# A macaron stack on one Trainium2 core: linear attention rewritten as one sequence of 128 query steps that also carries the projections, the FFN work and, on TensorE, a step's jobs ahead of its output products

## The reference

```
x = x + 0.5 * quant_ffn(layernorm(x))      # int8 weights and activations, 256 -> 256
x = x + linear_attn(layernorm(x))          # below
x = x + 0.5 * quant_ffn(layernorm(x))
x = x + 0.5 * routed_ffn(layernorm(x))     # top 128 of 1024 rows, 256 -> 1024 -> 256, gelu
x = x + attn(layernorm(x))                 # softmax, 16 heads of 128
x = x + 0.5 * routed_ffn(layernorm(x))
```

```
sq, sk = elu(q) + 1, elu(k) + 1
kv = einsum('bhsd,bhse->bhde', sk, v)
qkv = einsum('bhsd,bhde->bhse', sq, kv)
norm = einsum('bhsd,bhd->bhs', sq, sk.sum(axis=2))
return (qkv / (norm[..., None] + 1e-6)).transpose(...).reshape(b, s, H * D) @ Wo.T
```

## Time and profile before

| | us |
|---|---|
| Median of 3 runs | 3826.03 (3824.67 to 3826.09) |
| The profiled execution's own time | 3823.92 |
| Its span, from the first to the last instruction | 3822.3 |
| Setup | 0 to 18 |
| QA, four batches | 18 to 98.5 |
| Linear stage | 98.5 to 749.3 |
| Lead-in of attention (QB, FA and X of batch 0) | 749.3 to 883.1 |
| Attention's slots | 883.1 to 3722.6 |
| Tail, FB of batch 3 | 3722.6 to 3822.3 |

### The profile page before, as it was taken

One profiled execution on the slowest core, in us unless ns is written; L12 is line 12 of the kernel. 1 busy time (PEld: TensorE's weight loads), 2 busy tenths in 40 slices (PEclk: granted clock), 3 DMA queues, 4 the chain that ended last, 5 costly groups with the idle time before them and its releaser, 6 DMA issues.

```text
span 3822.3 us, 53962 instructions
## 1 busy us (share of the span) xinstructions
PE 3398.5 (89%) x19398; PEld 2873.2 (75%) x19398; DVE 2786.5 (73%) x5159; ACT 1984.8 (52%) x3557; POOL 1054.7 (28%) x1329
## 2 busy tenths in 40 slices
PE   2798898727999999999999999999999999999993
PEld 1687786626878888878887888878888788788873
DVE  7687877846777677776777767777677767776764
ACT  3455565423555556555555555555555465555551
POOL 4456564532112211212211221212212131112103
PEclk7899999958999999999999999999999999999996
DMA  1110100100000000000000001000000010000000
GB/s 48 47 33 20 33 23 24 33 21 18 12 12 20 28 13 12 12 13 24 26 12 13 21 23 35 15 12 20 27 12 13 13 31 29 13 20 25 24 6 28
DMA packets 78764, 82.84 MB, mean 22 GB/s; under 512 B 8016, under 2 KB 76240, under 8 KB 78416
## 3 DMA queue, kind: packets, MB, share of 16 engines
q1 hardware_dynamic: 78544, 79.89, 6.9%
HBM read 74.62 MB, written 5.24 MB: 21 GB/s over the span
## 4 chain that ended last, share of the span: by engine, by line
PE 63%; DVE 10%; ACT 5%; issue 2%; POOL 1%; DMA 0%; SPq 0%; DVEq 0%; POOLq 0%; ACTq 0%
PE at_ps_t L1725 12%; PE at_ps_job L35 6%; PE at_ps_job L37 6%; PE at_ps_job L36 6%; PE at_ps_o L37 5%; PE at_ps_o L35 5%; PE at_ps_o L36 5%; PE at_ps_s L35 5%; PE at_ps_s L37 5%; PE at_ps_s L36 5%; DVE at_probT_lo L1354 2%; ACT at_probT_hi L1227 1%; ACT x_resident L1343 1%; PE at_ps_job L1677 1%; DVE at_r L1501 1%
## 5 line engine op out<-in xcount | busy, mean ns | idle before, releaser
L1227 ACT ACTIVATE at_probT_hi<-at_ps_t 128x512 fp32r<-128x512 f32 x1024 | 611.5, 597 | 1155.0 <-PE at_ps_t L1725 1154.7
L1354 DVE TENSOR_TENSOR at_probT_lo<-at_ps_t,at_probT_hi 128x512 fp32r<-128x512 f32 x1024 | 705.3, 689 | 380.2 <-ACT at_probT_hi L1227 368.7
L1725 PE MATMUL at_ps_t<-ident,x_resident 128*128 128x128 f32 x4096 | 626.4, 276 | 102.9 <-DVE at_probT_lo L1354 92.3
L1725 PEld LDWEIGHTS at_ps_t<-ident,x_resident 128*128 128x128 f32 x4096 | 482.0, 141 | 255.6 <-DVE at_probT_lo L1354 114.6
L1583 DVE TENSOR_REDUCE at_neg_max<-at_ps_s 128x1 f32<-128x1024 f32 x512 | 622.8, 1216 | 10.2 <-PE at_ps_s L37 2.2
L1343 ACT ACTIVATE x_resident<-at_ps_s,at_neg_max 128x1024 f32<-128x1024 f32 x512 | 569.6, 1113 | 12.1 <-DVE at_neg_max L1583 7.7
L35 PE MATMUL at_ps_o<-at_probT_hi,at_v_lo 128*128 128x512 f32 x1024 | 445.5, 435 | 3.5 <-DVE at_oT_lo L1384 3.5
L35 PE MATMUL at_ps_s<-at_k_hi,at_q_lo 128*128 128x512 f32 x1024 | 446.4, 436 | 0.0
L1176 POOL TENSOR_TENSOR at_w_hi<-at_w_raw,at_cols 128x256 fp32r<-128x256 f32 x192 | 117.8, 614 | 1183.1 <-PE at_ps_job L37 1169.5
L37 PE MATMUL at_ps_o<-at_probT_lo,at_v_hi 128*128 128x512 f32 x1024 | 405.5, 396 | 0.0
L37 PE MATMUL at_ps_s<-at_k_lo,at_q_hi 128*128 128x512 f32 x1024 | 403.9, 394 | 0.0
(11 more groups left out here) (235 smaller groups left out, 7466.4 us busy)
## 6 DMA issues: line engine op xcount, KB each, us to landing
at_w_raw<-attn_w SPq DMA_DIRECT2D x256, 128.0 KB, 2.1
at_w_raw<-mlp_w SPq DMA_DIRECT2D x128, 128.0 KB, 2.4
li_wq_raw<-lin_q_w SPq DMA_DIRECT2D x64, 128.5 KB, 2.1
x_resident<-x SPq DMA_DIRECT2D x4, 1024.0 KB, 10.5
li_wo_raw<-lin_out_w SPq DMA_DIRECT2D x8, 512.0 KB, 3.6
li_xn<-lin_out_w SPq DMA_DIRECT2D x8, 512.0 KB, 4.0
out<-x_resident SPq DMA_DIRECT2D x4, 1024.0 KB, 5.1
li_z<-lin_kv_w SPq DMA_DIRECT2D x1, 1024.0 KB, 4.8
```

The lines of the kernel that those rows point to most:

```text
L1227: nc.scalar.activation(ph[:, i // TC, 4 * half:4 * half + 4, (i % TC) * P:(i % TC + 1) * P], ps_t[:], ACT.Copy).then_inc(s_ph, 1)
L1354: nc.vector.tensor_tensor(pl[at], ps_t[:], ph[at].bitcast(F32), ALU.subtract).then_inc(s_pl, 1)
L1725: last = nc.tensor.transpose(ps_t[:, j, :], prob[:, i % 2, kt * P:(kt + 1) * P], sh.ident[:])
```

## The change

The linear stage becomes one written-out sequence of steps t, from -32 to 133, the same on every engine; 128 of them, 0 to 127, are query steps, 32 for each batch without a break between batches. The other work of the stage is put at fixed steps, as are pieces of the FFNs:

- `linear_rows` places jobs. For batch b, 8 KV jobs of the first two key/value heads at 32b - 16 and on, 8 of the other two at 32b and on (each now 512 columns, a row tile's K and V of two heads; `kernel` reorders the weight for it), the sums at +11 and +12, turns at +13 and +14, and four products M at +15 to +21; the next batch's transposes (N) at 6, 8, 10 and 12 of the batch before.
- The chain of QA for batches 2 and 3, then QB, FA and X of batch 0 is placed in the same steps, by the same `Plan` as attention's background. QA of batch 2 lies at steps 0 to 19, QA of batch 3 at 20 to 41, QB at 42 to 59, FA at 60 to 117, X at 118 to 127. `quant_ffn_phase` keeps batches 0 and 1. Attention begins at step 0, with the QB chain of batch 3 three steps earlier than before (261, not 264). Its other places are the same or earlier by two or three.
- PE's step is query products, jobs, background, and last the output products of two steps before (`LAG` is 2, was 3). Three groups of two PSUM banks or four: `ps_q` 2, `ps_y` 4, `ps_job` 2.
- The norm moves from DVE to ACT (L1143). Of the four x updates DVE keeps three (L1255); ACT scales the fourth into `ybuf` (L1164) and POOL adds it. K's elu and low part are taken by two engines: DVE (L1241 and, for V, L1259), POOL for K. Transposes, FFN buffers and semaphores are shared with attention through a class `Chain`.

```diff
-def quant_ffn_phase(nc, sh, tag):
+def quant_ffn_phase(nc, sh, tag, batches):
...
+def linear_rows():
+    rows = {}
+    for b in range(B):
+        for p in range(2):
+            t = LOOP * b - H * (1 - p)
+            for i in range(TB):
+                rows.setdefault(t + i, []).append(("KV", 2 * b + p, i))
+            for j in range(2):
+                g = KVH * b + 2 * p + j
+                rows.setdefault(t + 11 + j, []).append(("SUM", g, 0))
+                rows.setdefault(t + 13 + j, []).append(("TURN", g, 0))
+                for i in range(2):
+                    rows.setdefault(t + 15 + 4 * j + 2 * i, []).append(("MADE", g, i))
+        for s, part in N_STEPS.items():
+            rows.setdefault(LOOP * (b - 1) + s, []).append(("N", b, part))
+    return rows
...
+    BEGIN, END = -LOOP, LOOP * B
+    plan = Plan(BEGIN, END + LAG + 2, lambda t: rows.get(t, []),
+                [("QA", 2, 0), ("QA", 3, 0), ("QB", 0, LOOP + LAG + 2), ("FA", 0, 0), ("X", 0, 3 * LOOP + 1)], [])
...
         @block.gpsimd
+            for t in range(BEGIN, plan.end):
+                if q_step(t - 1):
+                    k = t - 1
+                    pool.wait_ge(s_ph, k + 1)
+                    nc.gpsimd.tensor_tensor(pl[:, k % (LAG + 1), :], f[:, k % 2, :], ph[:, k % (LAG + 1), :].bitcast(F32),
+                                            ALU.subtract).then_inc(s_pl, 1)
+                if y_step(t - 1):
+                    m = t - 1 - LAG
+                    pool.wait_ge(s_y3, m + 1)
+                    x = x_tile_of(m, 3)
+                    nc.gpsimd.tensor_tensor(x, ybuf[:, m % 2, :], x, ALU.add).then_inc(s_x3, 1)
+                if t - 3 in kv_time:
+                    k, v, i = kv_time[t - 3]
+                    pool.wait_ge(s_kvh, k + 1)
+                    nc.gpsimd.tensor_tensor(kvl[:, i, 0:PK], z[:, k % 3, 0:PK], kvh[:, i, 0:PK].bitcast(F32),
+                                            ALU.subtract).then_inc(s_kl, 1)
+                if -2 <= t and t // 2 + 1 < B * H:
+                    (take_bias if t % 2 else split_wq)(t // 2 + 1)
...
+                pool_background(nc, pool, sh, c, t)
...
         @block.scalar
+            for t in range(BEGIN, plan.end):
+                evict(t)
+                act_evict(nc, act, c, t)
+                if q_step(t):
...
+                    nc.scalar.activation(f[:, t % 2, :], f[:, t % 2, :], ACT.Exp, scale=-1.0).then_inc(s_eq, 1)
+                if y_step(t):
+                    act.wait_ge(s_y, t - LAG + 1)
+                    nc.scalar.activation(norm[:], ps_y[:, :, D], ACT.Copy, bias=ATT_EPS).then_inc(s_norm, 1)
...
         @block.vector
-                        for j in range(TC):
...
-                            nc.vector.scalar_tensor_tensor(xt, ps_y[:, j, 0:D], rnorm[:, j:j + 1], xt,
-                                                           ALU.mult, ALU.add).then_inc(s_x, 1)
+                if q_step(t):
+                    dve.wait_ge(s_eq, t + 1)
+                    nc.vector.scalar_tensor_tensor(f[:, t % 2, :], ps_q[t % 2][:], bias[:, t // 2 % 2, 1:2], f[:, t % 2, :],
+                                                   ALU.add, ALU.max).then_inc(s_f, 1)
+                if y_step(t):
+                    m = t - LAG
+                    dve.wait_ge(s_norm, m + 1)
+                    if m:
+                        dve.wait_ge(s_y3, m)
+                    nc.vector.reciprocal(rnorm[:], norm[:]).then_inc(s_rn, 1)
+                    dve.wait_ge(s_rn, m + 1)
+                    for j in range(3):
+                        x = x_tile_of(m, j)
+                        nc.vector.scalar_tensor_tensor(x, ps_y[:, j, 0:D], rnorm[:, j:j + 1], x, ALU.mult, ALU.add).then_inc(s_x, 1)
...
         @block.tensor
+            for t in range(BEGIN, plan.end):
+                if q_step(t):
+                    if t % 2 == 0:
+                        pe.wait_ge(s_wql, t // 2 + 1)
+                    if t >= 2:
+                        pe.wait_ge(s_f, t - 1)
...
+                for kind, v, part in rows.get(t, []):
+                    job(kind, v, part)
+                pe_background(nc, pe, sh, c, t)
+                if y_step(t):
+                    m = t - LAG
+                    head = m // 2 % H
+                    pe.wait_ge(s_pl, m + 1)
...
 def build(nc, a, out):
-        quant_ffn_phase(nc, sh, "qa")
+        quant_ffn_phase(nc, sh, "qa", 2)
```

More of the change, by code:

```diff
@@ L257, in add @@
                     nc.gpsimd.tensor_tensor(xg, xg, y[:, 4 * i:4 * i + 4], ALU.add).then_inc(s_yfree, 1)
-            for g in range(B):
+            for g in range(batches):
                 rstd(g)
@@ new lines, in claim, with weight_unit, mlp_split @@
+def claim(pe, c, kind, v, part):
+    n = c.plan.place[kind, v, part]
+    if n >= 2:
+        by_act, count = c.plan.taker[n - 2]
+        pe.wait_ge(c.took if by_act else c.taken, count)
+    return c.ps_job[n % 2]
+def weight_unit(c, part, v):
+    if part == W1:
+        i = 2 * (v % 8 // 2 % 2) + v % 2
+        return (c.r1r[:, j * D:(j + 1) * D] for j in (i, 4 + i))
+    i = v % 2
+    return (c.r2r[:, j * D:(j + 1) * D] for j in (i, 2 + i))
+def mlp_split(part, v):
+    return 16 * (v // 8) + 8 * (part == W2) + v % 8 + 1
@@ new lines, in mlp_pieces, with mlp_source @@
+def mlp_pieces(c, t):
+    if t in c.plan.at and c.plan.at[t][0] in ROUTED:
+        kind, b, s = c.plan.at[t]
+        for part, steps in ((W1, W1_STEPS), (W2, W2_STEPS)):
+            if s in steps:
+                v = 8 * c.plan.no[kind, b] + 2 * steps.index(s)
+                yield part, v
+                yield part, v + 1
+def mlp_source(a, part, v):
+    if part == W1:
+        m, k = v % 8 // 2, v % 2
+        return a["mlp_w1"][:, k * DFF + m * D:k * DFF + (m + 1) * D]
+    return a["mlp_w2"][:, v % 8 * D:(v % 8 + 1) * D]
@@ new lines, in dve_statistics @@
+def dve_statistics(nc, dve, sh, c, kind, b, s):
+    no = c.plan.ln_no[kind, b]
+    if s == 0:
+        if kind == "FA":
+            dve.wait_ge(c.q_add, 4 * c.plan.no["QB", b] + 4)
+        elif kind == "X":
+            dve.wait_ge(c.taken, c.plan.by_dve["SC", c.plan.no["FA", b], 3])
+        else:
+            c.ready(dve, kind, b)
+    for j in range(3 * s, min(3 * s + 3, TB)):
+        nc.vector.bn_stats(sh.stats[:, j, :], c.x(b, j)).then_inc(c.ln.stats, 1)
+    if s == 2:
+        dve.wait_ge(c.ln.stats, TB * no + TB)
+        aggregate(nc, dve, sh, c.ln.mv, no)
```

1785 lines of the change are left out of this document (842 added, 943 removed).

## The result

The changed kernel takes 3952.12 us (median of 4 runs, 3949.62 to 3956.95) against 3825.35 for the kernel before (one run more than in the table above): a ratio of 1.0335, with a 95% interval of 1.0317 to 1.0353. It is 127 us slower, where 133 us faster was forecast.

What follows compares the result with a forecast made beforehand. It took four nearly equally full engines, coupled by the fixed step order, as the bound: 118.5 + 620 + 4 + 6 + 2939.2 + 1.5 = 3689.2 us span, 3692 as the run's time, range 3625 to 3765.

Steps and rivals of the forecast that it cites:

- Setup and quantised FFN, 58.5: First stage, two batches in place of four: it ends at 58.5 us, 40.0 less than before.
- Lead, 60: Start of the linear stage: 60 us of mostly serial transposes, KV jobs and sums, to the first query step at 118.5.
- The 128 steps, 620: Query steps of the linear stage: 620 us, 4.84 each, with four engines within 8% of each other.
- Sum of 605 from the busiest engine per step, less 28 for averaging: Query steps: largest of PE, DVE and ACT per class sums to 605 us; two steps of lag average out 28.
- 15 for the clock: Query steps: TensorE's clock at some 0.93, with TensorE busy 86%, adds 15 us.
- Waits where DVE and POOL work at once, +28: KV steps: two DVE operations each wait +0.5 us beside POOL, 56 in all, half hidden under PE.
- Hand-over, 6, and attention, 2940.7: After the steps' drain: 6 us to attention's first job, then 2939.2 for attention and 1.5 for a possible reload wait.
- B: Rival on the query steps: an elastic stream, fullest engine alone decides, steps of 4.3 to 4.5, 3617 to 3647; chance 0.22.
- C: Rival on the query steps: POOL and the shared port become the bound, 650 to 705 us, 3722 to 3777; chance 0.20.
- D: Rival on the query steps: gaps drop TensorE to its lower clock, slower than before, about 3910 at half; chance 0.05.
- break-even of 5.9 us a step: Query steps: at 754 us in all, 134 above the forecast, the change's gain is gone.

Runs made afterwards that it cites:

- e1: The changed kernel with TensorE's output products moved directly behind the query products, ahead of the step's jobs and background: 3748.04 us.
- e7: e6 with LAG = 3 in place of 2: 3735.59 us, ratio 0.9763 to the kernel before.
- e6: e1 with all four x tiles updated on VectorE, without ScalarE's scaled copy and GpSimd's addition: 3737.37 us.
- e5: e1 with the split of Wo on ScalarE and GpSimd moved from the end of a step to its beginning: 3791.42 us.
- e8: The changed kernel with eight idle matmuls put ahead of the jobs in query steps that have two or more: 3933.41 us.
- e2: The changed kernel with ScalarE's norm moved behind its high part of phi: 3916.83 us.

## Why the prediction was wrong, by its own steps

- **Setup and quantised FFN, 58.5:** 2.7 short. The next stage's first row is at 61.17, since GpSimd's last additions to x (4.64 from 56.22, two halves) ended the stage; the period of 40.0 that I took off was right only for its loop.
- **Lead, 60:** 121.7 - 61.2 = 60.5, and in part luck. The four transposes are 3.2 to 3.5 us apart (78.82, 82.33, 85.59, 88.82), as taken; but they begin 17.7 after the stage, not 15.5, the KV jobs take 13.9 and not 20, and from there to the first query product it is 16.5 and not 10, since the first sum waits 5.18 for GpSimd's low part of K.
- **The 128 steps, 620:** this is the step that failed, and in one sentence of it: "a step's maximum waits for its own query's two ACT passes, the copy for the maximum, POOL for the copy, and PE for POOL two steps later." The chain leaves out the norm. I had printed ScalarE's new order, with the norm ahead of the keys' passes and of phi, and TensorE's, with the jobs ahead of the output products, as the two things that moved, and gave neither a term: no cost for what the norm waits, and none for the claim of a job's bank, which is emptied only behind that norm. The account of what is queued behind a waiting instruction was owed for each edit and was not made for this one. What the order costs is now measured: 72 us in steps of one job and 141 in steps of two, 213 of the 260 by which the window exceeds the forecast, the lower clock's part included. The rest shows in e1: 5.20 a step in place of 4.84, 46 us.
- **Sum of 605 from the busiest engine per step, less 28 for averaging:** with the order turned round the 620 is 7% low. PE's work was 571.55 at a clock of 0.97, not 533 and 15 for the clock, 24 too few. Some of that is a slip in adding up: the four terms listed for PE (2.99 in 128 steps, 1.4 in 56, 2.9 in 14, and 45) make 547, not 533. Those listed for GpSimd make 482 of its 530, with no term for the splits of Wo (1.27 each); it measured 514.52. PE's share of 86.6%, forecast as 86%, came from two numbers that were both too small. I cannot say from these runs which of the small rings of e1 holds the remainder, only that the lag (e7) and the fourth x tile (e6) are not it.
- **Waits where DVE and POOL work at once, +28:** the mechanism was right, and the length of the operations fair for the order that runs well. V's low part on VectorE, least, median and most ns, in the changed kernel, and then V's low part and K's elu in e1:

```profile
L1259 DVE TENSOR_TENSOR li_kv_lo<-li_z,li_kv_hi x64: 411/417/2927, 98.2 to 898.9; 128x256 fp32r<-128x256 f32 x64
```
```profile
L1259 DVE TENSOR_TENSOR li_kv_lo<-li_z,li_kv_hi x64: 411/1004/2946, 98.5 to 701.4; 128x256 fp32r<-128x256 f32 x64
...
L1241 DVE SCALAR_TENSOR_TENSOR li_z<-li_z,li_ekk x64: 406/443/3822, 96.8 to 695.7; 128x256 f32<-128x256 f32 x64
```

  Where the engines take turns the median of V's low part is the least, where they overlap it is 0.59 above; that of K's elu is 0.04 above in e1. Summed over the 112 such operations in e1's steps they take 46 us more than their least, where 56 were counted. That half of this hides under PE is not shown. The Trainium skill ("SBUF — State Buffer", "Who interferes with whom") has the loser of the shared port pair wait for the other's whole instruction; the trace agrees with that in single cases (in e1 an addition of 4.55 us runs on GpSimd from 272.97 to 277.52, and the longest of VectorE's low parts of V, begun at 274.86, ends at 277.81). The 0.59 is about half of GpSimd's 1.3 for phi's low part, as a wait that begins at any time within it would be; this is an estimate, not a count.
- **Hand-over, 6, and attention, 2940.7:** 9.9 and 2939.9. The reload of batch 3, three steps nearer, cost nothing that shows.
- **The rivals:** B was refuted by every run with the whole work, of which e7 has the shortest steps, 5.11. C is not what made the changed kernel slow. Its price (3722 to 3777) happens to hold e1; there the port waits above are a part of the steps, but which part of the 40 us over the forecast they make was not told apart, and e6, with 87 us less of GpSimd's work in the steps (514 and 427), gained 11. D had the right sign for the wrong reason: the clock fell to 0.88, not to 0.5 in half of the steps, and the break-even of 5.9 us a step, which I worked out for it, was passed by waits at 6.88. The rival that was missing was the plain one: that the step's engines take turns. To any time slower than before I had given 0.04, all of it to D.

## What to carry to other kernels

When an edit puts work ahead of an instruction on one engine, follow that instruction's result to the engine that waits for it, and list all that is queued there behind the wait; if the moved work itself needs something from that queue (here a PSUM bank), the engines take turns, and a longer lag doesn't help, since both ends are in the same step. In a step that several engines share, issue first what others wait for, and last what only fills banks. Do the same for the queue that issues transfers (e5). A count of work per engine gives a floor; the sum needs the order's rings beside it, and in this kernel turning one block round was worth 204 us.

## What was not expected of the hardware

An 8-column operation of VectorE can be long beside GpSimd: the scales of a quantised batch, 128x8, took 2.25 us at 81.30 in the kernel before, while an addition of 4.50 us ran on GpSimd from 79.02, and 0.17 at 43.36, where none did. TensorE's granted clock in the steps was 0.88 at 73% busy in the changed kernel, 0.93 at 78% in e8 and 0.97 at 87% in e1; but e2, at 73% as well (608.70 of 830.30), had 0.92, so that the busy share of a stretch does not give its clock.
